# A four-layer GraphSAGE kernel: layer 1's own-feature products made early, one comparison for both one-hot sides, normalisation on VectorE

## The chip, the cores and the metric

The kernel runs on one core of one Trainium2 chip. The metric is device time in microseconds. Four compute engines work side by side, each through its own queue in order: TensorE (PE in the rows; PEld is its weight load), VectorE (DVE), ScalarE (ACT) and GpSimd (POOL). SyncE (SP) issues most of the DMAs. Engines wait for one another through semaphores only.

## The reference, cut to what matters

`x` is 3125 nodes by 256 features in fp32, with 50000 edges (`src`, `dst`), sorted by `dst`.

```python
def _sage_conv(x, src, dst, Wl, Wr, b):
    agg = jax.ops.segment_sum(x[src], dst, num_segments=n)
    deg = jax.ops.segment_sum(jnp.ones_like(dst, dtype=x.dtype), dst, num_segments=n)
    mean = agg / jnp.maximum(deg, 1.0)[:, None]
    return mean @ Wl + x @ Wr + b
h = jnp.maximum(_layernorm(x, axis=-1), 0.0)
h = relu(_sage_conv(h, ..., Wl1, Wr1, b1))      # 256 -> 256
h = relu(_sage_conv(h, ..., Wl2, Wr2, b2))      # 256 -> 128
h = relu(_sage_conv(h, ..., Wl3, Wr3, b3))      # 128 -> 256
return x + _sage_conv(h, ..., Wl4, Wr4, b4)     # 256 -> 256
```

## The kernel before, in words

The nodes lie in 25 tiles of 128; four tiles are a chunk of 512 (six full ones, and a last chunk with 53 nodes, "the tail"). The kernel works through the chunks as seven *places* `q` = 0 to 6, in the order `ORDER` = 5, 6, 4, 3, 2, 1, 0; place 1 is the tail. For each layer and place, TensorE sums the sources: 25 tiles of features `H` (fp16, in two parts, high and low) times a matrix `counts[source, target]` of edge counts, into two banks `agg_ps`, one for each half of the features (L2099, 98 matmuls of 512 columns in a full place).

**Making counts.** `counts` is built while layer 1 runs. Targets are taken in windows; a *step* is up to 128 edges of a window. For each step VectorE compares a row of numbers with the edges' sources (the one-hot `hot_src`, 128 wide) and with a key of target and source tile (`hot_key`, 100 wide for a narrow window, 200 for a wide one): two instructions at L1350 for a group of 4 steps (3 of wide windows). There is room for three groups (`GROUPS`). TensorE multiplies the two (L1928) into one of two window banks, and ScalarE copies each finished window pair into `counts` (L1674). The counts of the chunk of place `q + 1`, or a share of those of the last chunk, are made in place `q`. `script(q)` writes each place's order out for all three engines: a "sum" of one source tile for the first half of the features, a "half" for the second, and the steps spread between them over slots; a layer-1 product ("lin") counts as two slots in which steps may stand.

**Layer 1's linear part.** VectorE scales the sums by the inverse degree into `aggT` (L1444, `scale_agg`). The product of place `q - 1` is made in place `q` (`lin_part`, L1993): for each half `h` of the output two products of `W14[:, 0]` with `aggT` and two of `W14[:, 1]` with `selfT`, all in fp32 and 512 columns wide, in one accumulation in `lin_ps`; a product of 512 fp32 columns shows as two records. `selfT` is the chunk's own features, transposed, which SyncE loads from `hT_d[0]`. ScalarE then applies bias and relu from `lin_ps` (L1715), TensorE makes the narrow product for layer 2 (L2042), and ScalarE and VectorE split that in two parts of fp16.

**Own features.** The seven chunks of x are normalised first. VectorE (chunks in the first four of the order) or ScalarE (the others) makes the moments; ScalarE the root; VectorE `rstd` and `shift` (`h0_shift`); ScalarE one activation per tile, relu(x * rstd + shift) in fp32 in place (`h0_relu`, L1639, 25 tiles), and the high part in fp16 (`h0_high_part`, L1646); VectorE the low part (L1121). TensorE transposes the fp32 features through `ident32` (`h0_turn`, L1891), ScalarE copies them over the chunk's own x in SBUF (`h0_copy`, L1654), and SyncE stores them to `hT_d[0]`. In place 0 the chunks of places 0, 1 and 2 are turned, at tiles 14, 16 and 18; in place 1 the other four. `squares` (L1905), `turn_rows` (L1859) and the rank sums (L1830) also stand in place 0; they prepare bounds of layers 2 to 4 and the late step tables.

**A place's start.** Place `q` begins with the degrees: 100 small matmuls in places 0 and 2 (`add_degrees`, L2121), differences of step keys from place 3 on (`sum_cuts`, L2137). Its first "sum" writes the bank that `scale_agg` of place `q - 1` must have read.

## Time and profile before

| what | value |
|---|---|
| median of 3 runs | 684.47 us (682.58 to 685.35) |
| profiled execution, its own time | 683.4 us |
| its span | 681.6 us |
| mean granted TensorE clock | 0.985 of full speed |
| TensorE busy | 634.0 us, 93% of the span |
| VectorE, ScalarE, GpSimd busy | 283.5, 181.8, 39.1 us |
| the chain that ended last | PE 80%, DVE 10%, ACT 5%, issue 2%, DMA 1% |

All durations of rows are from one profiled execution; its time is 1.07 us under the median of the runs. Layer 1 with everything before it ends at about 327 us of the span; layers 2 to 4 fill the rest. In a row of the timeline, the first number is the start and the second the length; "[idle before <- who]" at its end is how long the engine had nothing to do, and who released it. A matmul's recorded length reaches into the next one, so what one costs is read from the spacing of the starts.

### The profile page before, as it was taken

How to read it: one execution, taken by the hardware profiler on the slowest of the kernel's cores; microseconds unless marked ns; L12 is line 12 of the kernel's file. 1: busy time of each engine (PE TensorE's matmuls, PEld its weight loads, DVE VectorE, ACT ScalarE, POOL GpSimd, SP SyncE). 2: the span in 40 equal slices, each digit the busy share in tenths (PEclk: the TensorE clock that was granted, in tenths of full speed). 3: DMA queues.
4: the chain of work that ended last, by engine and by line, in shares of the span. 5: the costliest groups of instructions: out<-in, count | busy, mean ns of one | idle time of the engine just before them, and what ended most of it. 6: DMA issues, size and time to landing. Idle time of an engine off the chain costs nothing.

```text
span 681.6 us, 10352 instructions
## 1 busy us (share of the span) xinstructions
PE 634.0 (93%) x4071; PEld 346.4 (51%) x4072; DVE 283.5 (42%) x775; ACT 181.8 (27%) x383; POOL 39.1 (6%) x91
## 2 busy tenths in 40 slices
PE   5558888999999999999999999899999999999998
PEld 4234545664554545554454444344445646546586
DVE  6986577478897978822112112121121110101011
ACT  3886882364642622310111110211220000000000
POOL 7000300000000000000000000000001020110110
PEclk9998997799999999999999999899999999999999
DMA  8300020610210111123234351334351123031130
GB/s 264 85 2 3 23 97 3 192 35 7 65 32 4 63 35 63 32 64 103 97 93 124 79 152 48 88 88 109 92 163 38 40 81 109 0 109 44 64 109 32
DMA packets 58727, 49.93 MB, mean 73 GB/s; under 512 B 31222, under 2 KB 44059, under 8 KB 58680
## 3 DMA queue, kind: packets, MB, share of 16 engines
q1 hardware_dynamic: 58324, 48.67, 25.0%
q8 instruction: 32, 0.52, 0.3%
q0 software_dynamic: 240, 0.37, 0.2%
q10 hardware_dynamic: 116, 0.24, 0.1%
q14 instruction: 15, 0.12, 0.1%
HBM read 27.10 MB, written 16.59 MB: 64 GB/s over the span
## 4 chain that ended last, share of the span: by engine, by line
PE 80%; DVE 10%; ACT 5%; issue 2%; DMA 1%; SPq 0%; DVEq 0%; POOL 0%; ACTq 0%; POOLq 0%
PE agg_ps L2099 30%; PE window_ps L2099 18%; PE lin_ps L1993 7%; PE window_ps L1928 6%; PE lin_ps L2017 5%; DVE early L1350 5%; PE lin_ps L2034 5%; ACT counts L1674 2%; PE window_ps L2075 2%; PE agg_ps L2075 2%; PE lin_ps L2042 1%; PE lin_ps L2121 1%; DVE rdeg L1429 1%; DVE aggT L1444 1%; ACT counts L1639 1%
## 5 line engine op out<-in xcount | busy, mean ns | idle before, releaser
L2099 PE MATMUL agg_ps<-counts,H 128*128 128x512 f16 (+3 forms) x1026 | 237.4, 360 | 0.9 <-DVE aggT L1444 0.8
L1350 DVE TENSOR_TENSOR early<-early 128x512 f16<-128x512 bf16 (+2 forms) x466 | 151.9, 389 | 26.5 <-PE window_ps L1928 25.0
L1928 PEld LDWEIGHTS window_ps<-early 128*128 128x128 f16 x892 | 69.6, 100 | 118.4 <-ACT counts L1674 37.1
L1928 PE MATMUL window_ps<-early 128*128 128x100 f16 (+1 forms) x892 | 101.4, 223 | 27.7 <-ACT counts L1674 13.9
L1674 ACT ACTIVATE counts<-window_ps 128x400 f16<-128x400 f32 x196 | 95.9, 504 | 108.5 <-PE window_ps L1928 104.8
L2099 PEld LDWEIGHTS agg_ps<-counts,H 128*128 128x128 f16 (+1 forms) x1026 | 80.8, 99 | 57.7 <-issue 11.0
L2099 PE MATMUL window_ps<-counts,early 128*128 128x512 f16 (+2 forms) x346 | 77.6, 379 | 0.0
L2099 PE MATMUL window_ps<-counts,H 128*128 128x512 f16 (+2 forms) x291 | 55.3, 347 | 0.0
L2099 PEld LDWEIGHTS window_ps<-counts,early 128*128 128x128 f16 (+1 forms) x346 | 33.7, 98 | 41.5 <-issue 3.2
L1452 DVE SCALAR_TENSOR_TENSOR partsT<-newT,columns,partsT 128x512 f16<-128x512 f32 (+1 forms) x21 | 14.4, 683 | 81.6 <-ACT partsT L1729 81.5
L1444 DVE SCALAR_TENSOR_TENSOR aggT<-agg_ps,columns,rdeg 128x512 f32<-128x512 f32 (+1 forms) x27 | 16.9, 658 | 72.7 <-PE agg_ps L2099 66.6
L2099 PE MATMUL agg_ps<-counts,early 128*128 (+4 forms) x297 | 46.5, 315 | 0.0
L2099 PEld LDWEIGHTS window_ps<-counts,H 128*128 128x128 f16 x291 | 24.9, 97 | 29.2 <-issue 1.5
L1715 ACT ACTIVATE newT<-lin_ps,columns 128x512 f32<-128x512 f32 (+1 forms) x28 | 17.3, 632 | 77.0 <-PE lin_ps L2034 45.4
L1031 POOL TENSOR_TENSOR newH<-newH,plan 128x256 f32<-128x256 f32 (+1 forms) x25 | 17.3, 724 | 353.8 <-DMA newH<-in_x_dram 353.8
L2099 PEld LDWEIGHTS agg_ps<-counts,early 128*128 128x128 f16 (+1 forms) x297 | 22.1, 97 | 24.3 <-issue 1.1
L1444 DVE SCALAR_TENSOR_TENSOR aggT<-window_ps,columns,rdeg 128x512 f32<-128x512 f32 (+1 forms) x13 | 9.0, 711 | 56.7 <-PE window_ps L2099 54.5
L1546 DVE TENSOR_TENSOR newT<-lin_ps,newH 128x512 f32<-128x512 f32 (+1 forms) x11 | 7.3, 667 | 51.5 <-PE lin_ps L2017 51.5
L1993 PE MATMUL lin_ps<-aggT,W 128*128 128x512 f32 (+1 forms) x56 | 27.1, 591 | 0.7 <-DVE aggT L1444 0.7
L1993 PE MATMUL lin_ps<-selfT,W 128*128 128x512 f32 (+1 forms) x56 | 25.5, 561 | 0.0
L1729 ACT ACTIVATE partsT<-newT,columns 128x512 f16<-128x512 f32 (+1 forms) x21 | 13.9, 664 | 33.7 <-DMA early<-partsT 18.4
L1715 ACT ACTIVATE newT<-newT,columns 128x512 f32<-128x512 f32 (+1 forms) x7 | 4.7, 667 | 65.8 <-DVE newT L1560 65.8
(218 smaller groups left out, 490.8 us busy)
## 6 DMA issues: line engine op xcount, KB each, us to landing
selfT<-hT_d SPq DMA_DIRECT2D x18, 512.0 KB, 4.3
hT_d<-newT SPq DMA_DIRECT2D x12, 512.0 KB, 4.6
rdeg<-rdeg_d SPq DMA_DIRECT2D x18, 256.0 KB, 4.3
counts<-in_x_dram SPq DMA_DIRECT2D x6, 512.0 KB, 8.1
hT_d<-counts SPq DMA_DIRECT2D x6, 512.0 KB, 3.9
newH<-in_x_dram SPq DMA_DIRECT2D x6, 512.0 KB
out_dram<-newT SPq DMA_DIRECT2D x5, 512.0 KB
hT_d<-newT SPq DMA_DIRECT2D x6, 256.0 KB, 4.0
```

The costliest lines, as they stand in the source:

```text
L1031: nc.gpsimd.tensor_tensor(x4[0:q, i, :], x4[0:q, i, :], b4rows[0:q, :], ALU.add).then_inc(x4_biased, 1)
L1350: last = v.tensor_tensor(hot[:, group % GROUPS, 0:n * size].rearrange("p (r n d) -> p r n d", r=n, d=2), numbers_to[:, 0:size].rearrange(" ...
L1444: v.scalar_tensor_tensor(out=aggT[:, h, 0:n], in0=(agg_ps, window_ps)[bank][:, h, 0:n], scalar=unscale[:, l - 1:l], in1=rdeg[:, 0:n], op0= ...
L1452: v.scalar_tensor_tensor(out=low, in0=(lin_ps if l == 1 else newT)[:, h, 0:n], scalar=scale[:, l - 1:l], in1=partsT[:, 0, 0:n], op0=ALU.mu ...
L1674: a.activation(counts[:, :, 2 * w * WIN:2 * (w + 1) * WIN].rearrange("p t (a w) -> p a t w", a=2), window_ps[:, FILL_AT[w] % 2, 0:2 * KEYS ...
L1715: a.activation(newT[:, h, 0:n], source, ACT.Relu, bias=bT[:, bias + h:bias + h + 1]).then_inc(relu_done[l], 1)
L1928: m(window_ps[:, at % 2, key0:key0 + keys], hot_src[:, group % GROUPS, r * P:(r + 1) * P], hot_key[:, group % GROUPS, r * keys:(r + 1) * k ...
L1993: last = m(lin_ps[:, h, 0:n], W14[:, i // 2, i % 2, h * P:(h + 1) * P], (aggT, selfT)[i // 2][:, i % 2, 0:n], start=(i == 0), stop=(i == 3))
L2017: last = m(lin_ps[0:rows_, g, i * D:(i + 1) * D], h, w, start=(j == 0), stop=(j == len(ops) - 1))
L2034: last = m(lin_ps[:, h, 0:n], w, r, start=(i == 0), stop=(i == len(ops) - 1))
L2075: last = m((agg_ps, window_ps)[bank][:, h, cols], tile[:, part, h * P:(h + 1) * P], counts[0:rows_, k, c * CH + g * HALF_CH:c * CH + (g + ...
L2099: last = m((agg_ps, window_ps)[bank][:, h, 0:n], tile[:, part, h * P:(h + 1) * P], counts[0:rows_, k, chunk_cols(c, n)], start=first and p ...
```

## The change

1. *Own products early.* `own_products(j)` makes the two-by-two products of `W14[:, 1]` with the own features right after the chunk is turned and copied: turn (tiles 1, 5, 9, 13, 17 of place 0), `h0_copy`, products (tiles 3, 7, 11, 15, 19), `own_copy` back over the chunk in SBUF, store. Places 0 to 4 of the order go in place 0, through `lin_ps`; the last two in place 1, through the window banks and `degree_ps`/`turn_bank`. `hT_d[0]`, and so `selfT`, now hold the mapped features.
2. `lin_part` keeps only the two products per half with `aggT`. VectorE adds the loaded `selfT` (`add_own`, at tile 4), writing `newT`; ScalarE's relu reads `newT`, a tile later than before.
3. *One comparison.* For narrow windows, source and key one-hots are both 128 wide and made by one instruction. From place 2 to place 4 (`SPREAD_FROM` to `SPREAD_TO`) they lie in rows of `counts` that belong to the last chunk, 8 steps in a group; elsewhere 4.
4. `ahead(q + 1)` makes the first two groups of places 3 and 4 before `scale_agg` of the place ahead of them.
5. *Normalisation.* VectorE makes x * rstd + shift per tile as one `tensor_scalar`; the relu is taken in the later readers (high part, low part, copy of the turned features).
6. `squares` and some small work is spread over other tiles; the degrees of place 0 must be read from `lin_ps` before the first turn.

```diff
+    SPREAD = 8
+    SPREAD_FROM = steps_of([w for q in range(-1, 2) for w in FILLS[q]])
+    SPREAD_TO = steps_of([w for q in range(-1, NCH - 2) for w in FILLS[q]])
...
-            if q == 1 and k in FIRST_LIN_K:
-                work += [("lin", 4 * FIRST_LIN_K.index(k) + j) for j in range(4)]
+            if q == 1 and k == FIRST_LIN_K:
+                work += [("lin", j) for j in range(4)]
             if q > 1 and k == LIN_K:
-                work += [("lin", j) for j in range(8)]
+                work += [("lin", j) for j in range(4)]
...
-        H0_TURN_K = (14, 16, 18)
-        SQUARES_K = (9, 10, 11)
+        IN_LIN = 5
+        H0_TURN_K, OWN_K = (1, 5, 9, 13, 17), (3, 7, 11, 15, 19)
+        SQUARES_K = (8, 11, 13)
...
-        H0_LATE_K = (1, 4, 7, 10)
+        H0_LATE_K, OWN_LATE_K = 1, (4, 5)
...
+                for i in range(t):
+                    v.tensor_scalar(x_in[c][:, i, :], x_in[c][:, i, :], rstd[:, c, i:i + 1], shift[:, c, i:i + 1],
+                                    ALU.mult, ALU.add).then_inc(h0_made, 1)
...
+            def ahead(q):
+                at = hots_after(q - 1)
+                for _ in range(GROUPS - 1):
+                    if SPREAD_FROM <= at < min(SPREAD_TO, hots_after(q)):
+                        step(*STEP_PAIR[at])
+                        at += HOTS[GROUP_OF[at]][1]
...
+                if wide < WIN:
+                    pairs = numbers_to[:, 0:P].rearrange("p (n d) -> p n d", d=2)
+                    v.tensor_tensor(
+                        hots_of(group).rearrange("p r a (n d) -> p r a n d", d=2),
+                        pairs.unsqueeze(1).unsqueeze(1).broadcast_to([P, n, 2, P // 2, 2]),
+                        step_both[:, at:at + n, :, :].unsqueeze(3).broadcast_to([P, n, 2, P // 2, 2]),
+                        ALU.is_equal).then_inc(hot_made, 1)
+                    return
...
+            def add_own(q):
+                n, t = size_of(chunk_at(q))
+                dve.wait_ge(self_loaded[1], 16 * (q + 1))
+                if q > 0:
+                    dve.wait_ge(hT_stored[1], 16 * q)
+                    dve.wait_ge(narrow_done, q)
+                for h in range(2):
+                    dve.wait_ge(lin_done[1], 2 * q + h + 1)
+                    v.tensor_tensor(newT[:, h, 0:n], lin_ps[:, h, 0:n], selfT[:, h, 0:n], ALU.add
+                                    ).then_inc(own_added, 1)
...
                     if kind == "summed":
+                        if 1 < q < NCH - 1:
+                            ahead(q + 1)
                         scale_agg(1, q, 0)
...
-            def h0_relu(j, tiles):
-                        a.activation(x_in[c][:, i, :], x_in[c][:, i, :], ACT.Relu, bias=shift[:, c, i:i + 1],
-                                     scale=rstd[:, c, i:i + 1]).then_inc(h0_made, 1)
...
-                    a.activation(x_T[c][:, f, 0:t * P], h0_ps(j)[f][:, 0:t * P], ACT.Copy, scale=1 / H0_SCALE
+                    a.activation(x_T[c][:, f, 0:t * P], h0_ps(j)[f][:, 0:t * P], ACT.Relu, scale=1 / H0_SCALE
                                  ).then_inc(h0T_copied, 1)
+            def own_copy(j):
+                act.wait_ge(own_done, 2 * j + 2)
+                for h in range(2):
+                    a.activation(x_T[c][:, h, 0:n], h0_ps(j)[h][:, 0:n], ACT.Copy).then_inc(own_copied, 1)
...
                 if j > 0:
-                    pe.wait_ge(h0T_copied, 2 * j)
+                    pe.wait_ge(own_copied, 2 * min(j, IN_LIN))
...
+            def own_products(j):
+                pe.wait_ge(h0T_copied, 2 * j + 2)
+                pe.wait_ge(weights_loaded, 16 * NW)
+                for h in range(2):
+                    for k in range(2):
+                        last = m(h0_ps(j)[h][:, 0:n], W14[:, 1, k, h * P:(h + 1) * P], x_T[c][:, k, 0:n],
+                                 start=(k == 0), stop=(k == 1))
+                    last.then_inc(own_done, 1)
...
                 if j == 0:
                     pe.wait_ge(agg_scaled[1], 2 * (q + 1))
-                    pe.wait_ge(self_loaded[1], 16 * (q + 1))
-                h, i = j // 4, j % 4
-                last = m(lin_ps[:, h, 0:n], W14[:, i // 2, i % 2, h * P:(h + 1) * P],
-                         (aggT, selfT)[i // 2][:, i % 2, 0:n], start=(i == 0), stop=(i == 3))
+                h, k = j // 2, j % 2
+                last = m(lin_ps[:, h, 0:n], W14[:, 0, k, h * P:(h + 1) * P], aggT[:, k, 0:n], start=(k == 0),
+                         stop=(k == 1))
```

How the instructions move on TensorE at the start of place 0, before (L2121 the degrees, L2099 sums, L1830 rank sums, L1928 steps):

```order
L2121 MATMUL lin_ps<-newH,counts 128x2 x100
L2099 MATMUL agg_ps<-counts,H 128x512 x8
L1830 MATMUL degree_ps<-counts,newH 128x512 x16
L2099 MATMUL agg_ps<-counts,H 128x512 x14
L1928 MATMUL window_ps<-early 128x200 x3
```

and of the changed program (L2201, L2179, L1895 and L2010 are the same lines; L1956 is the turn, L1968 the own products):

```order
L2201 MATMUL lin_ps<-newH,counts 128x2 x100
L2179 MATMUL agg_ps<-counts,H 128x512 x4
L1956 MATMUL lin_ps<-newH,counts 128x128 x8
L2179 MATMUL agg_ps<-counts,H 128x512 x4
L1895 MATMUL degree_ps<-counts,newH 128x512 x16
L2179 MATMUL agg_ps<-counts,H 128x512 x4
L1968 MATMUL lin_ps<-counts,W 128x512 x4
L2179 MATMUL agg_ps<-counts,H 128x512 x8
L1956 MATMUL lin_ps<-newH,counts 128x128 x2
L2179 MATMUL agg_ps<-counts,H 128x512 x2
L2010 MATMUL window_ps<-early 128x200 x3
```

One turn of eight transposes, one of two (the tail) and four products now stand ahead of the first step.

TensorE in place 1, before (L1891 turns, L1993 products of place 0, L2042 the narrow product):

```order
L1891 MATMUL degree_ps<-newH,counts 128x128 x4
L1891 MATMUL turn_ps<-newH,counts 128x128 x4
L2099 MATMUL agg_ps<-counts,H 128x53 x6
L1993 MATMUL lin_ps<-aggT,W 128x512 x2
L1993 MATMUL lin_ps<-selfT,W 128x512 x2
L2099 MATMUL agg_ps<-counts,H 128x53 x6
L1891 MATMUL window_ps<-newH,counts 128x128 x8
```

and changed (L1956 turns, L2073 products with the sums, L1968 own products, L2122 the narrow product):

```order
L1956 MATMUL window_ps<-newH,counts 128x128 x8
L1956 MATMUL degree_ps<-newH,counts 128x128 x4
L1956 MATMUL turn_ps<-newH,counts 128x128 x4
L2179 MATMUL agg_ps<-counts,H 128x53 x6
L2073 MATMUL lin_ps<-aggT,W 128x512 x4
L2179 MATMUL agg_ps<-counts,H 128x53 x6
L1968 MATMUL window_ps<-counts,W 128x512 x4
L2179 MATMUL agg_ps<-counts,H 128x53 x4
L1968 MATMUL degree_ps<-counts,W 128x512 x2
L1968 MATMUL turn_ps<-counts,W 128x512 x2
L2179 MATMUL agg_ps<-counts,H 128x53 x34
L2122 MATMUL lin_ps<-newT,Wl_sb 128x512 x2
```

The two last chunks are turned together, and their eight own products stand between the products of place 0 and the narrow product that waits for its relu.

VectorE in place 3, around the reading of the degrees, before (L1350 the comparisons, L1423 the degrees, L1429 a quarter of their inverses):

```order
L1423 SCALAR_TENSOR_TENSOR rdeg<-degree_ps,rdeg 128x512
L1350 TENSOR_TENSOR early<-early 128x512
L1350 TENSOR_TENSOR early<-early 128x400
L1350 TENSOR_TENSOR early<-early 128x512
L1350 TENSOR_TENSOR early<-early 128x400
L1350 TENSOR_TENSOR early<-early 128x512
L1350 TENSOR_TENSOR early<-early 128x400
L1429 RECIPROCAL rdeg<-rdeg 128x128
```

and changed (L1393 the comparison, L1507 the added own map):

```order
L1393 TENSOR_TENSOR counts<-early 128x8x256 x5
L1507 TENSOR_TENSOR newT<-lin_ps,selfT 128x512 x2
L1473 SCALAR_TENSOR_TENSOR rdeg<-degree_ps,rdeg 128x512
L1393 TENSOR_TENSOR counts<-early 128x8x256
L1479 RECIPROCAL rdeg<-rdeg 128x128
```

Four instructions of 512 and 400 elements have become one of 2048, and two additions stand in VectorE's queue behind the products of the place.

## Rows read from the trace of the kernel before

**Rows 1.** The page, parts 1 and 2: busy times; granted TensorE clock per fortieth

```profile
PE 634.0 (93%) x4071; PEld 346.4 (51%) x4072; DVE 283.5 (42%) x775; ACT 181.8 (27%) x383; POOL 39.1 (6%) x91
...
PEclk9998997799999999999999999899999999999999
```

**Rows 2.** Busy times by stretch: bounds, length, us (instructions) per engine, clock, DMA

```profile
15.00:47.00 32.00, 16.82 (x85) 6.66 (x86) 27.85 (x100) 26.12 (x65) 0.00 (x0) 1.00 0.26 67
47.00:105.00 58.00, 47.75 (x388) 28.00 (x386) 39.92 (x123) 43.82 (x109) 6.19 (x6) 0.97 0.12 37
105.00:126.00 21.00, 19.68 (x182) 13.27 (x183) 12.22 (x40) 6.69 (x14) 0.00 (x0) 0.84 0.25 90
...
168.00:209.00 41.00, 39.83 (x297) 20.66 (x296) 34.39 (x98) 20.09 (x41) 0.52 (x1) 1.00 0.14 41
...
251.00:292.00 41.00, 39.71 (x306) 21.04 (x305) 34.96 (x102) 10.29 (x20) 0.53 (x1) 1.00 0.15 41
292.00:327.00 35.00, 34.10 (x224) 16.81 (x224) 9.17 (x15) 2.06 (x3) 0.53 (x1) 1.00 0.29 87
```

**Rows 3.** Groups by line and shape: busy us, mean ns, idle before and releaser

```profile
L1674 ACT ACTIVATE counts<-window_ps 128x400 f16<-128x400 f32 x196 | 95.9, 504 | 108.5 <-PE window_ps L1928 104.8
L1350 DVE TENSOR_TENSOR early<-early 128x512 f16<-128x512 bf16 x199 | 83.1, 418 | 25.2 <-PE window_ps L1928 24.2
...
L1350 DVE TENSOR_TENSOR early<-early 128x400 f16<-128x400 bf16 x200 | 72.0, 360 | 0.0
...
L1639 ACT ACTIVATE counts<-counts,newH 128x256 f32<-128x256 f32 x25 | 13.5, 599 | 0.6 <-DVE newH L1112 0.6
...
L1546 DVE TENSOR_TENSOR newT<-lin_ps,newH 128x512 f32<-128x512 f32 x10 | 6.9, 692 | 46.8 <-PE lin_ps L2017 46.8
...
L1654 ACT ACTIVATE counts<-lin_ps 128x512 f32<-128x512 f32 x4 | 2.2, 599 | 0.0
```

**Rows 4.** TensorE's timeline, last place of layer 1: start, us, instructions

```profile
329.17 1.88 PE L1993 MATMUL lin_ps<-selfT,W 128*128 128x512 f32 x4
330.89 1.88 PE L1993 MATMUL lin_ps<-aggT,W 128*128 128x512 f32 x4
```

**Rows 5.** TensorE's timeline in place 0: a full place turned, and what follows

```profile
82.15 1.05 PE L1891 MATMUL lin_ps<-newH,counts 128*128 128x128 f32 x8
83.04 0.59 PE L2099 MATMUL agg_ps<-counts,H 128*128 128x512 f16 x2
```

**Rows 6.** Who waited for whom, 47 to 104 us: total, times, longest

```profile
PEld window_ps L1928 <- ACT counts L1674: 12.6, 14, 2.1
...
PE window_ps L1928 <- ACT counts L1674: 7.4, 7, 1.9
```

**Rows 7.** VectorE's timeline, ends of the first stretch and start of place 0

```profile
35.54 1.23 DVE L1121 TENSOR_TENSOR H<-counts,H 128x1024 f16<-128x1024 f32 x1 [1.53 <-ACT H L1646]
...
46.55 4.29 DVE L1132 TENSOR_SCALAR counts<-counts 98x512 f16<-98x512 f16 x16
50.76 0.15 DVE L1477 TENSOR_SCALAR newH<-lin_ps 128x4 f32<-128x4 f32 x1
```

**Rows 8.** One microsecond of place 0: busy times and granted clock

```profile
64.00:65.00 1.00, 1.00 (x6) 0.44 (x5) 1.00 (x11) 0.81 (x2) 0.00 (x0) 0.50 0.00 0
```

**Rows 9.** TensorE's timeline, place 1: products at half clock

```profile
108.89 3.28 PE L1993 MATMUL lin_ps<-aggT,W 128*128 128x512 f32 x4
112.01 1.88 PE L1993 MATMUL lin_ps<-selfT,W 128*128 128x512 f32 x4
```

**Rows 10.** TensorE's timeline where place 3 begins

```profile
167.67 0.59 PE L2099 MATMUL agg_ps<-counts,H 128*128 128x512 f16 x2
168.94 0.29 PE L1928 MATMUL window_ps<-early 128*128 128x100 f16 x3 [0.68 <-DVE early L1350]
```

**Rows 11.** Line 1350 alone, by stretch: VectorE's busy us and instructions

```profile
168.00:209.00 41.00, 28.46 (x88) 1.00 0.14 41
```

**Rows 12.** VectorE's timeline in place 1: one fp32 tensor and a constant

```profile
107.14 0.29 DVE L1293 TENSOR_SCALAR counts<-counts 128x256 f32<-128x256 f32 x1
```

186 lines of the change are left out of this document (111 added, 75 removed).

## The prediction

> **What bounds the kernel now.** I read the page first: TensorE is busy 634.0 of 681.6 us [rows 1], and its clock is full nearly everywhere. So a gain must come from TensorE work that goes, or from work that moves into its 47 idle us. The table by stretch [rows 2] shows where these lie. The first stretch (15 to 47 us) has TensorE half idle, with VectorE busy 27.85 and ScalarE 26.12 of 32 us: these two bound it, hand in hand. Place 0 (47 to 105) has TensorE busy 47.75 of 58, place 1 19.68 of 21. Places 3 and 5 have it busy 39.83 and 39.71 of 41, place 6 34.10 of 35: here TensorE is the bound. VectorE comes next in places 3 and 5 (34.39 and 34.96 of 41); in place 6 it does little. The waits of place 0 [rows 6] say who holds TensorE there: ScalarE's window copies, 7.4 us in 7 pieces. Last I read the timeline at a place's start [rows 10]: the first step waits 0.68 us for VectorE's one-hots, which were not begun before the sums were scaled.
>
> **What the change does to TensorE's sum of work: nothing.** Four of eight fp32 products per place leave `lin_part` and four own products come in. A group of four records, two products, starts 1.72 us before the next [rows 4], so one product is 0.86 and four are 3.44 us. The tail's four short ones move too, from place 2 to place 0, and cancel. So the question is only how much of 6 x 3.44 = 20.6 us finds idle time.
>
> **First stretch: +0.5 us.** Nine tiles are normalised by VectorE instead of ScalarE. No row shows this instruction. The nearest is one fp32 tile of 256 with a constant, 0.29 us [rows 12]; the other end is the activation it replaces, 0.599 [rows 3]. I take 0.29, the same tile on the same engine: nine cost VectorE 2.6 us, and ScalarE is relieved of nine activations. VectorE's wait of 1.53 us for ScalarE's high part [rows 7] then goes, because that chain loses four activations; 2.6 - 1.5 = 1.1, of which I let other waits hide half. Bounds: -1.5 (the activations were the path) to +3.9 (nine at 0.599 less the 1.5).
>
> **Place 0: +10.6 us.** Added on TensorE: own products of four full chunks, 4 x 3.44 = 13.8, and two more turns of full chunks (five instead of three; one is 0.89 [rows 5]), 1.8; together 15.6. Ahead of the first step two new waits stand in TensorE's queue. The first turn waits for the degrees to be read from `lin_ps`. VectorE reads them at 50.76, behind the 16 comparisons of 4.29 us [rows 7], and now four normalisations (1.2) stand ahead of those: I take 0.9 us, since the sums of tile 0 cover the rest. Everything of TensorE's place is queued behind it. The first products wait for `h0_copy(0)`, 2 x 0.6 [rows 3], which stands behind ScalarE's copy of the ranks: 0.8 after the four sums between. So 1.7 us of new waits. Against that stands the old idle: 58 - 47.75 = 10.2 [rows 2], of which 1.9 (the branch over heavy windows at the end) stays, so 8.3. ScalarE gets lighter by 16 activations of 0.54 to 0.6 (9) and heavier by own copies (3.5 pairs, 4) and two more copy pairs (2): it falls from 43.82 to about 41 us over a longer place. The later windows are thus stored in time more often. I let 3.3 of the 8.3 us stay, for the new handshakes turn, copy, product, copy, each some 4 to 5 us of TensorE time apart. The half-clock stretch after the longest gap [rows 8] I take as gone, since products now fill that gap: -1.7. Sum 15.6 + 1.7 + 3.3 - 8.3 - 1.7 = +10.6. Bounds: nothing hidden and the waits on top, 15.6 + 1.7 + 3.3 = 20.6; all idle filled and no waits, 15.6 - 8.3 - 1.7 = 5.6.
>
> The rows show that half clock (0.50, that is 1.2 GHz, against 2.4) at 64 us, a little after the engine had stood still, and it was back soon after dense work [rows 8]. The Trainium skill (TensorE: Matmul & The Clock Gate, "Part 1: The HAM clock gate") says that the throttled clock is the default and activity releases it; by that rule denser place 0 and 1 would run at full clock, and the sum would be better by up to the 1.4 us of the group in [rows 9]; by the row alone place 1 stays as it is.
>
> **Place 1: +2.0 us.** `lin_part` loses 3.44, two own product groups add 6.88, two turns fewer give back 1.8: +1.7. The relu of place 0 moves behind both own copies in ScalarE's queue, and the narrow product waits for it: +0.9. TensorE no longer waits for ScalarE between four single turns: -0.6 (not in the rows, an estimate from the 0.6 of one copy). The half clock stays: four records took 3.12 us there instead of 1.72 [rows 9], after the idle at place 0's end. Bounds 0 to +5.
>
> **Places 2 to 6 and the start of layer 2: -17.2 us.** Products of places 2 to 6 are full ones, halved where TensorE is the bound: five times 3.44 (made in places 3 to 6 and behind place 6). Added behind them is VectorE's `add_own`, an fp32 sum from PSUM like L1546's 0.69 [rows 3], so 1.4 us, then relu and narrow product. In places 3 to 6 some six tiles of sums stand between the products and the narrow one and cover it; at layer 2's start 1.5 us do, and about 0.1 shows. DVE's queue holds steps behind the addition, but up to 24 steps are made ahead, twice as many as before. Cost taken: 0.
>
> **One comparison: VectorE stays under TensorE.** 44 pairs in place 3 took 28.46 us [rows 11], 0.647 a pair. From the two shapes [rows 3], 0.418 - 0.360 us for 112 elements, 0.52 ns each; a pair's 912 elements are 0.474, leaving 0.086 an instruction. One of 2048 is then 1.15 us, 22 of them 25.3: 3.1 less. With 1.4 for the addition VectorE has 34.4 - 3.1 + 1.4 = 32.7 us of work, and TensorE 41 - 3.4 = 37.6. In place 5 groups hold 4 steps: 1024 elements, 0.62, 47 times saves only 1.3, and 35.0 stand against 37.6, with the wait for the last sums besides: I charge 1.0 there. The Trainium skill (VectorE: DVE Perf Modes, "Side-by-side: where the cycles go for N=2048 bf16") gives each instruction a fixed part of some 150 cycles; by it 66 fewer instructions would save some 10 us of VectorE in each of these places. The spacing of the rows shows 0.086 us, so the trace does not bear that out for instructions that follow one another; TensorE's time would not change by either.
>
> `ahead` takes away the 0.68 us of [rows 10] at the starts of places 3 and 4: -1.4. Place 2 has no such help, and its first one-hots are 0.4 us later: +0.4.
>
> **Sum.** 0.5 + 10.6 + 2.0 - 17.2 + 1.0 - 1.4 + 0.4 = -4.1 us. The profiled execution took 683.4, giving 679.3; the median of the runs is 1.07 above it, so 680.4 us.
>
> **Rivals.**
> *Place 0 swallows it all.* ScalarE's relief matters more than I think, all of the old idle is filled, and place 5 is not held: 5.0 less for place 0 and 1.0 for place 5, -10.1, 674.4 us. For it: 8.3 us of idle are there, nearly all of it behind ScalarE [rows 6]. Against: TensorE waits for ScalarE in order, and the copies of own products add new such points.
> *The handshakes serialise (the other side).* Each own product group waits for `h0_copy`, and that stands in ScalarE's queue behind window copies, moments and high parts. If each of the six full groups waits 1.6 us beyond my sum, two window copies and one of the turned ones (2 x 0.504 + 0.6 [rows 3]), this costs 9.6: +5.5, 690 us. The place is TensorE's queue at tiles 7 to 19 of place 0 and 4 and 5 of place 1; it decides from 1.2 us per group on, where 7.5 us cancel the gain and take half a per cent. For it: ScalarE is busy 43.82 of 58 us in place 0. Against: two tiles of sums and steps lie between turn and product.
> *The places become VectorE's.* The halved products don't shorten places 2 to 5 in full, because VectorE is in order and now also waits for the products: a loss of 1.5 in each of four places, +1.9 in all, 686.4, no change. For it: 34.96 of 41 us busy [rows 2].
> *The merged comparison does not keep its rate.* At half of it, 1.04 ns an element, 22 instructions are 48.8 us and the place some 56: four such places cost about 70 us, 750. Against: the innermost pairs are as before.
>
> **Chances.** My forecast 0.40; place 0 swallows it 0.25; handshakes 0.16; VectorE's places 0.16; the comparison 0.03. A measurement of this kernel tells about 0.5%, 3.4 us, from no change; so faster means under 681.1. Of my forecast's own range, 677 to 684, six tenths lie there: 0.24, with 0.25 of the first rival and a little of the third, 0.51. Same: 0.16 of mine and 0.14 of the third, 0.30. Slower: 0.16 + 0.03, 0.19. The range reaches from below the first rival to the handshakes: 672 to 690.
>
> **What would show it.** In the profile after: place 0 10 us longer and TensorE's idle there under 6 us; waits of L1968 for ScalarE's copies small (a sum over 8 us speaks for the handshakes); places 3 and 4 at 37 to 38 us; the 2048-element comparison at 1.2 us; VectorE's normalisation near 0.3 us; no gap at the first step of places 3 and 4; place 6 and the start of layer 2 shorter by 3.4 each; layers 2 to 4 unchanged. It is wrong if place 0 grows by over 16 us or by under 6, or if places 3 to 5 do not shorten by 3 us.

## The result and the profile after

The changed kernel takes 687.91 us (median of 6 runs, 687.37 to 689.92), the kernel before 684.03 (6 runs): a ratio of 1.0067, 95% interval 1.0053 to 1.0081. The whole interval lies above 1, so the change makes the kernel slower. The forecast was 680.4 us and faster. The range, 672 to 690, holds the measured time. The profiled execution took 687.79 us, its span is 686.0. The experiments below were run in four batches; the median of the kernel before, 22 to 30 runs in each batch, stayed at 683.7 to 683.9 us, so medians of different batches can be compared.

The page of the changed kernel, parts 1 and 2, where [rows 1] stood:

```profile
PE 635.7 (93%) x4071; PEld 348.0 (51%) x4072; DVE 292.3 (43%) x547; ACT 176.4 (26%) x372; POOL 40.8 (6%) x91
...
PEclk9999999989999999999999999899999999999999
```

TensorE does the same work in as many matmuls. VectorE is busy 8.8 us longer with 228 instructions fewer. So the 4.4 us of span must have come through place, order or clock, and the table by stretch says where. First the kernel before, cut at the starts of places 0 to 2 (their first degree matmuls) and then at the scalings that end places 2 to 6 and the first of layer 2 (columns as in [rows 2]):

```profile
46.67:104.95 58.28, 48.03 (x394) 28.27 (x395) 40.25 (x124) 44.09 (x109) 6.19 (x6) 0.97 0.12 37
104.95:125.89 20.94, 19.62 (x178) 13.21 (x179) 12.11 (x40) 6.69 (x14) 0.00 (x0) 0.84 0.24 88
125.86:166.77 40.91, 40.15 (x403) 24.66 (x403) 30.34 (x95) 19.87 (x42) 0.00 (x0) 0.92 0.21 53
166.77:208.02 41.25, 40.01 (x297) 20.67 (x296) 34.64 (x97) 20.09 (x41) 0.52 (x1) 1.00 0.14 41
208.02:250.11 42.09, 40.02 (x295) 20.87 (x294) 34.85 (x97) 18.98 (x38) 0.52 (x1) 1.00 0.13 40
250.11:291.67 41.56, 40.37 (x312) 21.39 (x311) 35.52 (x103) 10.29 (x20) 0.53 (x1) 1.00 0.15 41
291.67:325.72 34.05, 33.23 (x222) 16.60 (x222) 8.22 (x14) 2.06 (x3) 0.53 (x1) 1.00 0.30 89
325.72:354.36 28.64, 27.92 (x156) 13.24 (x155) 5.04 (x8) 3.51 (x5) 0.00 (x0) 1.00 0.31 94
354.36:681.60 327.24, 320.44 (x1656) 174.07 (x1654) 46.67 (x76) 25.42 (x40) 17.33 (x25) 0.99 0.30 83
```

and the changed kernel at the same events:

```profile
46.77:122.27 75.50, 65.84 (x450) 37.28 (x450) 46.16 (x119) 42.27 (x107) 7.26 (x6) 1.00 0.09 28
122.27:144.23 21.96, 19.97 (x169) 12.47 (x170) 13.41 (x42) 6.75 (x14) 0.00 (x0) 0.92 0.33 123
144.20:184.01 39.81, 38.91 (x395) 23.55 (x395) 30.85 (x33) 19.94 (x42) 0.00 (x0) 0.91 0.14 33
184.01:221.92 37.91, 36.76 (x289) 19.65 (x288) 33.76 (x33) 20.17 (x41) 0.52 (x1) 1.00 0.16 44
221.92:260.07 38.15, 36.72 (x287) 19.48 (x286) 31.09 (x31) 18.88 (x38) 0.53 (x1) 1.00 0.14 44
260.07:300.15 40.08, 37.15 (x304) 19.84 (x303) 35.95 (x57) 10.35 (x20) 0.52 (x1) 1.00 0.16 42
300.15:330.76 30.61, 29.79 (x214) 15.05 (x214) 9.61 (x15) 2.13 (x3) 0.53 (x1) 1.00 0.33 100
330.76:356.10 25.34, 24.71 (x147) 11.61 (x146) 6.42 (x10) 3.57 (x5) 0.00 (x0) 1.00 0.33 106
356.10:686.00 329.90, 321.98 (x1656) 175.10 (x1654) 46.67 (x76) 25.42 (x40) 17.34 (x25) 0.99 0.30 82
```

| stretch | before | after | difference | forecast |
|---|---|---|---|---|
| up to place 0 | 46.67 | 46.77 | +0.1 | +0.5 |
| place 0 | 58.28 | 75.50 | +17.2 | +10.6 |
| place 1 | 20.94 | 21.96 | +1.0 | +2.0 |
| places 2 to 6, start of layer 2 | 228.5 | 211.9 | -16.6 | -17.2 |
| the rest of layers 2 to 4 | 327.24 | 329.90 | +2.7 | 0 |

Two rows miss by much: place 0 by 6.6 us, and by 2.7 us a stage that the change does not touch. That stage lasted 327.1 to 330.8 us over the seventeen profiles of this study, kernels with and without own products near both ends, so its 2.7 us are within the scatter of single profiles. So is the 0.1 of the first row: place 0 began at 46.0 to 47.5 us in the fifteen profiles of kernels that have no own products ahead of it. In place 0 the reader is to compare two columns. TensorE's busy time grew by 17.8 us, 48.03 to 65.84. Its idle time, length less busy time, was 10.25 and is 9.66. Next to none of the old idle was filled.

The front of place 0 on TensorE after the change; before, the first step (L1928) stood at 59.96, 13.3 us behind the start of the place:

```profile
50.14 1.89 PE L2179 MATMUL agg_ps<-counts,H 128*128 128x512 f16 x4
52.74 1.97 PE L1956 MATMUL lin_ps<-newH,counts 128*128 128x128 f32 x8 [0.71 <-DVE newH L1541]
54.50 1.91 PE L2179 MATMUL agg_ps<-counts,H 128*128 128x512 f16 x4
56.21 4.79 PE L1895 MATMUL degree_ps<-counts,newH 98*128 98x512 f16 x16
60.83 1.03 PE L2179 MATMUL agg_ps<-counts,H 128*128 128x512 f16 x4
62.75 3.70 PE L1968 MATMUL lin_ps<-counts,W 128*128 128x512 f32 x8 [0.89 <-ACT counts L1713]
```

The first step now comes at 68.66. The turn takes 1.76 us here (52.74 to 54.50) and 0.89 later in the place [rows 5]; the 16 rank sums (L1895) take 4.62 us, where they took 3.52 before. The turn is slow at this spot in every profile that has it there. The rank sums are not slow because of the turn: they took 3.45 to 4.62 us in the six profiles with a turn ahead of them and 3.45 to 4.65 in the eleven without. The own products (eight records, four products) take 3.54 us, since the next sum starts at 66.29: 0.1 more than the four products of [rows 4].

TensorE's waits in place 0 after, which answer to [rows 6]:

```profile
PE window_ps L2010 <- ACT counts L1741: 4.9, 5, 2.4
PE lin_ps L2201 <- issue: 1.6, 1, 1.6
PE lin_ps L1968 <- ACT counts L1713: 1.3, 2, 0.9
PE lin_ps L2201 <- ACT counts L1741: 1.2, 1, 1.2
PE lin_ps L1956 <- DVE newH L1541: 0.7, 1, 0.7
PE lin_ps L1956 <- ACT counts L1722: 0.7, 2, 0.4
PE lin_ps L1968 <- issue: 0.2, 1, 0.2
```

(Its columns are the total, the times and the longest.) Window waits fell from 7.4 us behind ScalarE and 1.0 behind VectorE to 4.9; the new handshakes of turns and products cost 2.9 (1.3 + 0.7 + 0.7, and 0.2 of issue). The two rows of L2201 are the degrees at the start and end of the place; the kernel before has them too, 1.2 and 1.7.

The price of VectorE's new instructions, in the groups by line and shape:

```profile
L1393 DVE TENSOR_TENSOR counts<-early 128x2048 f16<-128x2048 bf16 x65 | 77.5, 1215 | 6.5 <-PE window_ps L2010 6.3
...
L1143 DVE TENSOR_SCALAR counts<-counts,newH 128x256 f32<-128x256 f32 x25 | 8.9, 416 | 0.3
```

The comparison of 2048 elements takes 1.2 us on the mean, and 22 of them in place 3 have 26.3 us for the 25.3 forecast. The normalisation (L1143) is 0.416 on the mean; four of them in a row took 1.38, 0.35 a piece, not 0.29.

### The profile page after: what moved, and what is told of

Read it like the earlier page. It is cut to its first block, busy times and chain, and to the rows that moved or that the text cites. A ratio compares the mean times of both kernels' runs of the same rounds, so it can differ in the third digit from the quotient of the medians.

```text
span 686.0 us, 10095 instructions
## 1 busy us (share of the span) xinstructions
PE 635.7 (93%) x4071; PEld 348.0 (51%) x4072; DVE 292.3 (43%) x547; ACT 176.4 (26%) x372; POOL 40.8 (6%) x91
## 4 chain that ended last, share of the span: by engine, by line
PE 81%; DVE 10%; ACT 5%; issue 2%; POOL 1%; DMA 1%; SPq 0%; DVEq 0%; ACTq 0%; POOLq 0%
PE agg_ps L2179 30%; PE window_ps L2179 19%; PE window_ps L2010 5%; PE lin_ps L2097 5%; PE lin_ps L2114 5%; PE lin_ps L2073 3%; PE lin_ps L1968 2%; ACT counts L1741 2%; DVE early L1400 2%; PE lin_ps L2122 2%; DVE early L1393 2%; PE window_ps L2155 2%; PE agg_ps L2155 2%; PE degree_ps L1895 1%; DMA early<-partsT 1%
## 5 line engine op out<-in xcount | busy, mean ns | idle before, releaser
L2179 PE MATMUL agg_ps<-counts,H 128*128 128x512 f16 (+3 forms) x1026 | 238.8, 359 | 0.9 <-DVE aggT L1494 0.8
L2179 PEld LDWEIGHTS agg_ps<-counts,H 128*128 128x128 f16 (+1 forms) x1026 | 80.2, 99 | 59.8 <-issue 14.1
L1393 DVE TENSOR_TENSOR counts<-early 128x2048 f16<-128x2048 bf16 x66 | 78.4, 1211 | 6.5 <-PE window_ps L2010 6.3
L2179 PE MATMUL window_ps<-counts,early 128*128 128x512 f16 (+2 forms) x346 | 77.6, 379 | 0.0
L2010 PE MATMUL window_ps<-early 128*128 128x100 f16 (+1 forms) x366 | 47.0, 238 | 23.1 <-DVE early L1400 13.0
L2010 PEld LDWEIGHTS window_ps<-counts 128*128 128x128 f16 x526 | 40.3, 99 | 48.7 <-issue 9.8
L2010 PEld LDWEIGHTS window_ps<-early 128*128 128x128 f16 x366 | 28.8, 101 | 60.3 <-ACT counts L1741 25.5
L2010 PE MATMUL window_ps<-counts 128*128 128x100 f16 x526 | 52.6, 211 | 3.1 <-ACT counts L1741 2.0
L2179 PE MATMUL window_ps<-counts,H 128*128 128x512 f16 (+2 forms) x291 | 55.3, 347 | 0.0
L2179 PEld LDWEIGHTS window_ps<-counts,early 128*128 128x128 f16 (+1 forms) x346 | 33.6, 98 | 41.5 <-issue 3.2
L1393 DVE TENSOR_TENSOR early<-early 128x1024 f16<-128x1024 bf16 (+1 forms) x69 | 43.8, 681 | 17.8 <-PE window_ps L2010 17.4
L2179 PE MATMUL agg_ps<-counts,early 128*128 (+4 forms) x297 | 46.5, 315 | 0.0
L2179 PEld LDWEIGHTS window_ps<-counts,H 128*128 128x128 f16 x291 | 24.9, 97 | 29.2 <-issue 1.5
L1787 ACT ACTIVATE newT<-newT,columns 128x512 f32<-128x512 f32 (+1 forms) x21 | 13.4, 663 | 89.9 <-DVE newT L1628 65.8
L2179 PEld LDWEIGHTS agg_ps<-counts,early 128*128 128x128 f16 (+1 forms) x297 | 22.1, 97 | 24.3 <-issue 1.1
L2073 PE MATMUL lin_ps<-aggT,W 128*128 128x512 f32 (+1 forms) x56 | 25.1, 564 | 0.6 <-DVE aggT L1494 0.6
```

What stands on the lines that cost most here:

```text
L1393: v.tensor_tensor(hots_of(group).rearrange("p r a (n d) -> p r a n d", d=2), pairs.unsqueeze(1).unsqueeze(1).broadcast_to([P, n, 2, P // 2 ...
L2010: m(window_ps[:, at % 2, key0:key0 + keys], one_src, one_key, start=(j == 0), stop=(j == STEPS[w] - 1)).then_inc(hot_used, 1)
L2073: last = m(lin_ps[:, h, 0:n], W14[:, 0, k, h * P:(h + 1) * P], aggT[:, k, 0:n], start=(k == 0), stop=(k == 1))
L2179: last = m((agg_ps, window_ps)[bank][:, h, 0:n], tile[:, part, h * P:(h + 1) * P], counts[0:rows_, k, chunk_cols(c, n)], start=first and p ...
```

## The experiments

Each ran beside the kernel before. "Place 0" below is the profiled execution's, from one profile each. Two kernels with the TensorE order of the kernel before showed 61.2 us there at a mean clock of 0.94 instead of 58.28 at 0.97, so single profiles of place 0 are sure to some 3 us only; the medians decide.

**e1, part 1 undone.** `lin_part` with eight products again, turns at 14, 16, 18, no `own_products`, `own_copy` and `add_own`; parts 3, 4 and 5 stay.

```diff
-                work += [("lin", j) for j in range(4)]
+                work += [("lin", j) for j in range(8)]
...
-        H0_TURN_K, OWN_K = (1, 5, 9, 13, 17), (3, 7, 11, 15, 19)
+        H0_TURN_K = (14, 16, 18)
...
-                        own_products(OWN_K.index(k))
...
-                        add_own(q - 1)
```

> The changed kernel with its part 1 undone: own products again in lin_part (eight products a place), turns at tiles 14, 16, 18 of place 0, relu from lin_ps; the one comparison, the groups made ahead and the normalisation on VectorE stay. Theory A (place 0 takes the moved TensorE work at its full price, and the other parts are nearly neutral): place 0 is back at 58 to 60 us instead of 75.5, places 3 and 4 end up 0.7 shorter each than in the kernel before, all in all 682 to 684 us, 4 to 6 under the changed kernel. Theory B (the loss is VectorE's: nine normalisations more in the first stretch, four ahead of the degrees, the larger comparisons): place 0 stays at 63 us or more and the whole at 686 to 689. Theory C (the prediction's own sum for the rest: first stretch +0.5, place 5 +1.0, ahead -1.4, place 2 +0.4, front waits none): 684.5.

Measured: 681.25 us (12 runs), ratio to before 0.9967 (0.9946 to 0.9989). Place 0 is 57.07 us:

```profile
47.46:104.53 57.07, 48.26 (x394) 28.50 (x395) 45.56 (x118) 36.77 (x93) 6.39 (x6) 0.97 0.12 37
```

Theory A holds, and its numbers were a little too high: 681.25 for 682 to 684, 57.07 for 58 to 60. Part 1 costs 6.7 us (687.91 - 681.25), more than the whole loss, and the other parts gain 2.6. From scaling to scaling places 3 and 4 took 40.24 and 40.74, 1.0 and 1.3 under the kernel before, place 5 41.34.

**e2, half of each own product left out.** The kernel computes the own map from 128 of the 256 features.

```diff
-                    for k in range(2):
-                        last = m(..., W14[:, 1, k, ...], x_T[c][:, k, 0:n], start=(k == 0), stop=(k == 1))
+                    last = m(..., W14[:, 1, 0, ...], x_T[c][:, 0, 0:n], start=True, stop=True)
```

> The changed kernel with half of each own product left out (the second 128 of the 256 features; two products instead of four per chunk). Everything else, copies and waits too, is as changed. It takes 1.77 us from each of six full chunks: 7.1 in place 0, 3.5 in place 1. Theory A (nothing in place 0 covers the own products): place 0 falls from 75.5 to about 68.4, place 1 by 3 to 3.5, the whole by 10 to 677.5. Rival (the products stand in idle time that comes back when they go): place 0 falls by less than 4, the whole to 681 or more.

Measured: 677.16 us, 10.75 under the changed kernel for 10.6 of work taken out. This median of 6 runs is sure to some 2 us only (ratio to before 0.9916, 0.9884 to 0.9948). The profile is sharper: place 0 is 68.11 us, 7.4 shorter for 7.1 taken out, and TensorE's idle time in it is 9.76 us, where it was 9.66. Theory A: this work had no cover that can be seen. The waits show why. TensorE's timeline of the changed kernel, two of the rows that begin with a wait:

```profile
62.75 3.70 PE L1968 MATMUL lin_ps<-counts,W 128*128 128x512 f32 x8 [0.89 <-ACT counts L1713]
...
94.35 0.22 PE L2010 MATMUL window_ps<-early 128*128 128x100 f16 x1 [2.35 <-ACT counts L1741]
```

and of e2:

```profile
62.49 1.98 PE L1967 MATMUL lin_ps<-counts,W 128*128 128x512 f32 x4 [0.89 <-ACT counts L1713]
...
90.22 0.22 PE L2009 MATMUL window_ps<-early 128*128 128x100 f16 x1 [2.36 <-ACT counts L1741]
```

The waits are the same to a hundredth of a microsecond, and so are those of 0.89, 0.35, 0.33, 0.37, 0.44 and 0.61 us between and behind them. One is not: 0.72 us for a window copy at 114.37 became 0.46, and 0.41 for VectorE came ahead of it. If TensorE's work had been filling time in which ScalarE was behind, less of it would have made the waits longer by some 7 us. All but one of them don't depend on how much TensorE does. My reading: what it waits for begins only after an instruction of its own.

**e3, the first turns later**, the first one behind the rank sums; ScalarE's copies follow.

```diff
-        H0_TURN_K, OWN_K = (1, 5, 9, 13, 17), (3, 7, 11, 15, 19)
+        H0_TURN_K, OWN_K = (3, 6, 9, 13, 17), (5, 8, 11, 15, 19)
```

> The changed kernel with the first two turns and own products later: turn of place 0's chunk at tile 3 (behind the rank sums) instead of 1, its products at 5 instead of 3, the tail's at 6 and 8 instead of 5 and 7. Theory A (the front loses by a wait of 0.7 us and by half speed that lasts longer: the turn took 1.76 instead of 0.89, the 16 rank sums 4.6 instead of 3.4): eight sums and 16 rank sums run as in the kernel before, first step at 65.5 to 66 us instead of 68.66, the whole 2.5 to 3 us faster, 685. Rival (the front's length is the work that stands in it, and ScalarE's burst behind the rank sums only moves): within 0.7 us of the changed kernel, 687.5.

Measured: 687.09 us, ratio to before 1.0050 (1.0031 to 1.0070). TensorE's timeline at the front of place 0:

```profile
50.15 3.59 PE L2179 MATMUL agg_ps<-counts,H 128*128 128x512 f16 x8
...
58.79 1.04 PE L1956 MATMUL lin_ps<-newH,counts 128*128 128x128 f32 x8
...
65.25 0.42 PE L2010 MATMUL window_ps<-early 128*128 128x200 f16 x3
```

The turn is back at 0.87 us, both waits are gone and the first step stands at 65.25, 3.4 earlier. The rank sums still took 4.39 us, where theory A had them as before, at 3.5. But the place ends only 0.6 earlier (74.92 us): behind the front TensorE waits 6.2 us for window copies instead of 4.9, and some half clock comes in (mean 0.98). The front was short as theory A has it, but not by the faster rank sums; the gain was given back, and the time is the rival's.

**e4, ScalarE's queue in another order**: `h0_copy(0)`, five moment pieces and a root ahead of `first_rows`, which waits for the ranks.

```diff
-   2: (h0_root(4), first_rows(3, ...), h0_copy(0)),
+   2: (h0_root(4), h0_copy(0), h0_moment(5, 1), h0_moment(5, 2), h0_moment(5, 3),
+       h0_root(5), h0_moment(6, 0), h0_moment(6, 1), first_rows(3, ...)),
```

> The changed kernel with ScalarE's queue in another order in place 0: the copy of the first turned chunk and six moment pieces stand ahead of the rank row, for which ScalarE waited 10.3 us; TensorE's order is as changed. Theory A (TensorE's waits in place 0 are bursts of ScalarE's queue behind that wait): the 0.9 us wait of the first own products goes, the 2.35 us wait near 94 us shrinks, together 1.5 to 3 us faster, 685 to 686.5. Rival (those waits come from windows finishing one after the other and not from the burst): only the 0.9 goes and half of it comes back, 687 to 688.

Measured: 686.76 us, 1.0042 (1.0024 to 1.0059), between the two. The wait of 0.9 went; the one of 2.35 stayed (2.36), against theory A. Place 0 was 72.44 us, 3.1 shorter, but this profile is of the fastest of 12 executions (682.15 us), and 1.65 of the 3.1 are busy time: the half speed at the front ended sooner (rank sums in 3.45 us with the turn where it was). What ScalarE did in the wait of 2.35, in the changed kernel:

```profile
91.49 1.06 ACT L1705 ACTIVATE H<-counts 128x1024 f16<-128x1024 f32 x1
92.44 0.42 ACT L1687 ACTIVATE counts<-counts 128x256 f16<-128x256 f32 x1
...
92.98 0.51 ACT L1689 ACTIVATE counts<-counts 128x256 f16<-128x256 f32 x1
...
93.61 0.30 ACT L1698 ACTIVATE newH<-counts 128x4 f32<-128x4 f32 x1
93.82 0.88 ACT L1741 ACTIVATE counts<-window_ps 128x400 f16<-128x400 f32 x2
```

A high part, a moment piece and a root stand between two window copies at tile 13, and e4 had left them there.

**e15, one piece out of that burst.**

```diff
-   10: lambda: h0_copy(2), 12: ...,
-   13: lambda: (norms(2), h0_high_part(5), h0_moment(6, 3), h0_root(6)),
+   10: lambda: h0_copy(2), 11: lambda: h0_moment(6, 3), 12: ...,
+   13: lambda: (norms(2), h0_root(6), h0_high_part(5)),
```

> The changed kernel with one edit in ScalarE's queue of place 0: a moment piece (1.25 us) from tile 13 to tile 11, and the root ahead of the high part, so that the burst between two window copies is shorter by the piece. Theory A (the wait is the length of the burst): the 2.35 us wait near 94 us becomes 1.1, every other wait keeps its length, place 0 is 1.2 shorter (74.3). Rival (it is only moved to tile 11): place 0 stays at 75.5.

TensorE's timeline of e15:

```profile
93.01 0.22 PE L2010 MATMUL window_ps<-early 128*128 128x100 f16 x1 [1.19 <-ACT counts L1741]
```

Measured: 686.02 us, 1.9 under the changed kernel; place 0 74.10. The 2.35 became 1.19, less by the piece, and each of the other waits kept its length to 0.05 us. So this wait is as long as the burst in ScalarE's queue; for the shorter ones that was not tried one by one.

**e13 and e14, the bursts out of place 0**, with and without own products: moments ahead of the rank row and at tiles 5 and 7 (without own products: all of them around the rank row), `square_weights` on VectorE at tile 4 instead of 6; in e13 the turns as in e3.

```diff
-   4: lambda: (h0_low_part(3), h0_shift(4)), 6: square_weights,
+   4: lambda: (h0_low_part(3), h0_shift(4), square_weights()),
...
-   13: lambda: (norms(2), h0_high_part(5), h0_moment(6, 3), h0_root(6)),
+   13: lambda: (norms(2), h0_high_part(5)),
```

> The changed kernel with the bursts of place 0 spread: all moment pieces but two and a root ahead of the rank row in ScalarE's queue, the last two pieces at tiles 5 and 7, so that at tile 13 only the high part stands between two window copies; VectorE squares the weights at tile 4, while it waits for the ranks; the first turn and its products behind the rank sums. Theory A (TensorE's idle in place 0 is set by the order of the other queues, and is taken away piece by piece): the 2.35 us wait falls to about 0.8, the front as in the run with the later turn, 683 to 685, 3 to 5 under the changed kernel. Rival (waits are shared out anew): 686 to 687.5.

> The changed kernel with its part 1 undone, and the same spreading of ScalarE's moments and of the squared weights. Its place 0 showed waits of 1.42 and 0.36 us behind the squared weights on VectorE, 1.91 behind ScalarE's high part with a moment piece and a root. Theory A: both shrink to under 0.6, 2 to 3 us less than without the moves (680.9): 678 to 679. Part 1 in e13 still costs 4 or more against this run, since its work lies on the path wherever it stands in place 0. Rival (the bursts were what made part 1 expensive): e13 comes within 2 us of this run.

Measured: e13 683.88 us (ratio 1.0002, 0.9983 to 1.0020), e14 677.53 (6 runs, 0.9909, 0.9878 to 0.9941). Both times are theory A's, e14's even a little below its range; the waits shrank less than it says. In e13 the 2.35 became 1.00 and a new one of 1.53 us for a window copy stands at 68.43; in e14 e7's 1.91 became 1.00, its 1.42 is gone, and VectorE is waited for 1.09 us at 84.06. e14's place 0 is 53.48 us long, against 57.07 in e1, and of these 3.6 us only 2.0 are idle time. The other 1.6 are busy time: the mean clock of the place is 1.00 instead of 0.97, so the half clock that e1 has behind its waits is gone. Reordering was worth 4.0 us with the own products and 3.7 without (681.25 - 677.53). Part 1 still costs 6.4 (683.88 - 677.53): not the bursts made it dear. e14 is the fastest kernel of the study that does the whole work, 0.9% under the one before and 1.5% under the changed one.

**e7**, an early form of e14 with three moment pieces and a root moved only.

```diff
-   2: (h0_root(4), first_rows(3, ...)),
+   2: (h0_root(4), h0_moment(5, 1), h0_moment(5, 2), h0_moment(5, 3), h0_root(5), first_rows(3, ...)),
```

> The changed kernel with its part 1 undone, as in the first run of this study (681.25 us), and ScalarE's three moment pieces and a root moved ahead of the rank row for which it waits. Theory A (window waits of place 0 are bursts of ScalarE behind that wait): 1 to 3 us less than that run, 678.5 to 680. Rival (waits there come from the windows' own rhythm): 681 within 0.7.

Measured: 680.88 us (0.9965, 0.9946 to 0.9984), 0.4 from e1: the rival's number. It had left the burst at tile 13 and the squared weights in place, and the waits of 1.91 and 1.42 behind them.

**e5 and e6, own products ahead of place 0**, between the windows of the first stretch, where TensorE was half idle: two places' (e5), three places' (e6).

```diff
+        EARLY = 2
+        EARLY_TURN = {17: 0, 25: 1}
+        EARLY_OWN = {19: (0, 0), 20: (0, 1), 21: (0, 2), 22: (0, 3), 27: (1, 0, 1, 2, 3)}
-        H0_TURN_K, OWN_K = (1, 5, 9, 13, 17), (3, 7, 11, 15, 19)
+        H0_TURN_K, OWN_K = (9, 13, 17), (11, 15, 19)
...
+                    pe.wait_ge(own_copied, 2 * EARLY)
```

The keys are windows, the numbers behind them places and products. Both also have ScalarE's moments ahead of the rank row, as e4 has.

> The changed kernel with the own products of the first two places of the order (one full chunk and the tail) moved ahead of place 0, between the windows of the first stretch, where TensorE stood idle for 15 of 32 us; the full chunk's four products one by one behind four windows. ScalarE's queue in place 0 as in the run with another order, less these copies. Theory A (place 0 has no cover, the first stretch has): place 0 loses a turn of 0.9, products of 3.5, the tail's 1.1, and with them the wait and the half speed of the front (about 2.8), 8 us in all against the changed kernel's, first stretch at most 1 us longer: 679 to 680.5. Rival (the first stretch hangs on VectorE and ScalarE hand in hand, and each burst of TensorE pushes the windows back): the stretch grows by 3 or more, 683 or more.

> As the run with two early places, with the third place's chunk too (turn behind window 26, its four products behind windows 28 to 31). Theory A: another 0.9 + 3.5 = 4.4 us from place 0, first stretch up to 1.5 longer for the last products, since little stands behind them: 675.5 to 677.5. Rival: its products and copies stand where nothing covers them and the degrees wait for the copy: no gain over the run with two, 679 to 682.

Measured: e5 686.09 us (1.0035, 1.0022 to 1.0048), e6 684.94 (1.0020, 1.0000 to 1.0040). Place 0 began at 51.32 and 55.20 us instead of 46.77, and lasted 70.7 and 63.0. Of the 4.8 and 12.5 us by which place 0 was shorter, 4.5 and 8.4 came back in the first stretch. e5 went the rival's way. e6 lies above both expectations, since neither allowed for so long a stretch. New waits stood there too, in e5 1.40 us for the copy of the turned chunk, and turns took 1.54 us. Half clock came on top: in e5 the granted clock was 0.50 from 44 to 59 us, and the mean of place 0 was 0.89 (e6: 0.95) instead of 1.00. What of the miss is order and what is clock was not separated. That TensorE's idle in that stretch is of the same kind as in place 0, a waiting for others that wait for it, fits the runs and is not shown by them alone.

**e8, the addition of the own map cut to 4 of 512 columns from place 2 on.**

```diff
-   v.tensor_tensor(newT[:, h, 0:n], lin_ps[:, h, 0:n], selfT[:, h, 0:n], ALU.add
+   v.tensor_tensor(newT[:, h, 0:4 if q > 1 else n], lin_ps[:, h, 0:4 if q > 1 else n], ...
```

> The changed kernel with the addition of the own map cut to 4 of 512 columns for the places from 2 on: 1.2 us less of VectorE in each of places 3 to 6 and at the start of layer 2. Theory A (place 5 is VectorE's, places 3 and 4 are not): place 5 (40.1 us from scaling to scaling) shortens by 1.0 to 1.3, places 3 and 4 (37.9 and 38.2) by less than 0.4, start of layer 2 by 0.5 or less: 686 to 686.7. Rival (places 3 and 4 hang on VectorE too): each shortens by 1, 684.5.

Measured: 687.31 us. Place 5 took 39.02 us instead of 40.08, places 3 and 4 37.91 and 38.01 instead of 37.91 and 38.15. So place 5 hangs on VectorE, places 3 and 4 do not: theory A. The whole is 0.6 under the changed kernel where 1.2 to 1.9 were expected, which a median of 7 runs doesn't settle. Its place 0, where nothing was changed, was 76.68 us in this profile and 75.50 in the changed kernel's.

**e12, parts 3 and 4 alone**, normalisation on ScalarE.

> The kernel before with parts 3 and 4 alone: the one comparison, groups of 8 from place 2 to place 4, two groups made ahead; normalisation stays on ScalarE. Theory A (the 2.6 us by which the kernel without own products is faster than the one before come from the starts of places 3 and 4 and from fewer waits for comparisons): 681 to 682. Rival (half of it is ScalarE's relief by the normalisation on VectorE, in place 0): 682.5 to 683.5.

Measured: 682.78 us, 0.9987 (0.9970 to 1.0004). From place 3 to place 6 its lengths are e1's within 0.01 us (40.23, 40.74, 41.34, 34.05), so the gain of places 3 and 4 is parts 3 and 4. The whole is the rival's number. The 1.5 us between e12 and e1 would then be part 5's, but the two intervals overlap, and the mean clock of place 0 (0.94 against 0.97) may be all of it: what part 5 is worth was not shown.

**The gap in layer 3.** The 2.7 us of the last row of the table come from one place, the tail of layer 3, on TensorE before and after:

```profile
438.01 0.42 PE L2034 MATMUL lin_ps<-aggT,plan 128*128 128x53 f32 x2 [3.14 <-DVE aggT L1444]
```

```profile
440.93 0.67 PE L2114 MATMUL lin_ps<-aggT,plan 128*128 128x53 f32 x2 [4.66 <-DVE aggT L1494]
```

TensorE waits for VectorE, VectorE for ScalarE's high part, and that for the DMA transposition of the part before, which took 8.89 us before (from 431.40) and 10.41 after (from 432.80). Half clock follows the gap, 3.4 us of it before and 6.8 after. e9, e10 and e11 are e1, the changed kernel and the kernel before with VectorE's scaling of the tail put ahead of the low part that waits for that high part.

```diff
-                    scale_agg(l, q, bank)
+                    if not (l == 3 and q == 1):
+                        scale_agg(l, q, bank)
...
                     for h in range(TURNS[l]):
+                        if l == 3 and q == 0 and h == 1:
+                            scale_agg(3, 1, 1 - bank)
                         low_part(l, q, h)
```

> The changed kernel with its part 1 undone, and in layer 3 the scaling of the tail's sums ahead of the second low part of the first place in VectorE's queue (behind it, it waits for a DMA transposition: TensorE stood still for 3.1 to 4.7 us there and then ran at half clock for 3 to 7 us, in every profile so far). Theory A (TensorE's gap there hangs on that place in VectorE's queue alone): gap gone and with it most of the half clock, 4 to 6 us less than without the swap (681.25): 675.5 to 677.5, and runs that lie closer together. Rival (something behind it waits for the same DMA, so the gap only moves): 680 or more.

> The changed kernel with the same swap in layer 3. Theory A (of the measured loss of 3.9 us, layer 1 and the start of layer 2 account for 1.7, and the rest is this gap, which fell out 1.5 us longer with more half clock): 682 to 684, and 1.2 to 2.4 above the kernel before with the same swap. Rival (the gap is as long in both kernels over many runs; the loss lies elsewhere): the distance to the kernel before with the swap stays at 3.5 or more.

> The kernel before with the same swap in layer 3. Its gap was 3.14 us and the half clock behind it took some 1.6 more. Theory A: 4 to 5 us less than the kernel before, 679 to 680.5. Rival (the gap only moves): 683.5.

Measured: 681.75, 690.54 and 685.12 us (ratios 0.9968, 1.0089, 1.0007). The gap moved to the next instruction that needs the same DMA, TensorE's turn of the tail, and grew: 5.1, 6.4 and 5.0 us. Theory A falls in all three, and with it my reading that 2.7 of the 4.4 us were this gap's accident: with the swap the changed kernel is 5.4 us above the kernel before, not the 1.2 to 2.4 expected (e10's profile has half clock in place 6, worth 1.7 us, see below; it would not close the distance). Over the profiles of this study the first transposition took 8.9 to 9.3 us in five kernels (before, e2, e4, e9, e11) and 10.1 to 10.6 in the other twelve, with and without own products in both kinds. What decides between the two stays open.

## Why the prediction was wrong

**The step that failed** is place 0, forecast +10.6 us and measured +17.2, and it failed in two terms: 2.7 of the 6.6 us are idle time that was not filled, 3.9 are work.

*The idle time.* "I let 3.3 of the 8.3 us stay" treated TensorE's idle of place 0 as room: ScalarE is behind, so more TensorE work lets it catch up. Measured, idle went from 10.25 to 9.66 us, where the sum (less 8.3, plus 3.3 kept, plus 1.7 of new waits) has 7.0. e2 shows that the moved products had no cover, and e15 that the longest wait there is as long as the burst that stands in ScalarE's queue between two window copies. Window waits did fall, by 3.5 us, and 2.9 of handshakes took their place.

*The work.* The sum had 15.6 us less 1.7 of half clock, 13.9; busy time grew by 17.8. The first turn at half speed is 0.9 of the difference. The tail's own products are another 0.9, which the prediction let cancel against place 2 (place 2 is indeed 1.1 shorter). The products' 3.54 instead of 3.44 are 0.4. The slower rank sums are 1.1, but that is luck of these two profiles and not the change: with and without a turn ahead of them they took 3.5 to 4.6 us. That leaves 0.6 unaccounted. The 1.7 of half clock at 64 us did go, as forecast: the clock is 1.00 there. But the prediction looked for half speed only where [rows 8] recorded it; at the front of the place, into which the first turn moved, the spacing of the first eight sums shows it (below).

**Front waits:** 0.9 and 0.8 were forecast, 0.71 and 0.89 measured. The half speed of the turn behind the first was missed.

**First stretch:** +0.1 for +0.5, although an instruction cost 0.35 and not 0.29. The same first stretch was 0.7 us longer in e1's profile, so this agreement says little.

**Place 1:** +1.0 for +2.0. Its mean clock is 0.92 instead of 0.84, where the prediction kept [rows 9]'s half clock.

**Places 2 to 6 and layer 2's start:** -16.6 for -17.2 (with 1.0 and -1.4 and 0.4 in it). Place 6 and the start of layer 2 gave 3.44 and 3.30, place 4 3.94 for 4.1, place 3 3.34 for 4.1. Against e1 the halved products gave places 3 and 4 only 2.3 and 2.6 each. TensorE's busy time fell by 2.8 and 2.9 there, not 3.4, and its idle time grew by 0.5 and 0.3: two waits for window copies of 0.56 and 0.42 stand in place 3, where e1 has one of 0.40 for VectorE. Place 4 has the same two, but e1 has two of 0.42 and 0.50 there as well. Why the busy time fell by less was not looked into.

Place 6 was luck in part. In four of the ten profiles with the own products made early (e3, e10, e13, e15) it lasted 32.30 us instead of 30.61, with the same waits: the clock fell to half behind a long run of matmuls of four columns (L2217), and TensorE had stood still only for the 0.82 us at the place's start that all ten have. Without early own products it was 34.04 or 34.05 us at full clock in all seven. Part 1 gives 3.4 us back there in some executions and 1.7 in others. The same six microseconds of place 6, in the tables by stretch, first in the changed kernel, then in e15:

```profile
312.00:318.00 6.00, 6.00 (x27) 2.83 (x26) 2.73 (x4) 0.00 (x0) 0.00 (x0) 1.00 0.65 222
```

```profile
311.14:317.14 6.00, 6.00 (x23) 2.43 (x22) 2.73 (x4) 0.00 (x0) 0.00 (x0) 0.75 0.67 223
```

Place 5 gave 1.5 for 2.4, VectorE's bound as forecast but larger:

```profile
PE window_ps L2010 <- DVE early L1393: 2.5, 5, 0.9
```

Those are TensorE's waits for VectorE between 260.07 and 300.15; in the same place of e1 they are 0.8 us.

**The comparison and `ahead`:** right. The 42 comparisons of 2048 elements of places 3 and 4 (two more are made ahead, in place 2) took 49.6 us, 1.18 each for 1.15 forecast, and the gaps of [rows 10] are gone there; in e1, without part 1, the two places are 1.0 and 1.3 shorter for 0.7 each.

**The rivals.** "Place 0 swallows it all" is the forecast's error made larger. "The places become VectorE's" came nearest in time (686.4), and that is luck: its mechanism is true of place 5 alone, as e8 shows. "The handshakes serialise" came next (690), and its mechanism is not what happened either: 2.9 us of such waits in place 0, where its sign was a sum over 8. That the range holds the measured time is owed to the handshake rival's number alone. What was missing is the plainest rival: that work added to place 0 costs its full price. On the sum of the prediction, with none of the old idle filled, that is 8.3 - 3.3 = 5.0 us more, 685.4.

**Why moved work costs at all.** By the medians part 1 costs 6.7 us (after against e1) and 6.4 (e13 against e14). By the two profiles of after and e1 it is 18.4 more in place 0 and 0.8 in place 1, and 13.8 less behind (0.9, 2.3, 2.6, 1.3, 3.4 and 3.3 in places 2 to 6 and at the start of layer 2): 5.4. In these two profiles the rows account for it: places 3 to 5 gave back 6.2 of the 10.3 us that left them (+4.1), the handshakes are 2.9, the half speed at the front 2.0; against that stand 2.0 less of window waits (4.9 after, 6.9 in e1) and 1.7 less of half clock. Sum 5.3. Of the front's 2.0 only the turn's 0.9 belongs to part 1. Over the whole span the two profiles are 3.9 us apart and the medians 6.7: e1's profile is of the slowest of its 12 executions, and place 6 is at full clock in both. So the medians give the size of part 1's cost, the profiles its kinds, and how much each kind has of the 6.7 stays open.

## What to carry to other kernels

Idle time of an engine is room only if what it waits for would go on without it. Look at what its releaser did in the gap: where that is a burst between two of the releaser's own duties, begun after the waiter's last instruction, more work for the waiter fills nothing, and the burst is what to move. Leaving half of an added piece of work out and comparing the waits one by one tells the two apart in a single experiment.

## What the runs showed of the hardware that was not expected

*Half speed that the clock column does not show.* Behind the 100 degree matmuls of two columns, eight sums of 512 columns took 3.39 us before, 0.42 a piece, while the granted clock of these microseconds is recorded as 1.00; the sixteen rank sums behind them, up to 56.94, took 0.22 a piece. In e5 the same eight sums, where the clock is recorded as 0.50, took 3.38. TensorE's timeline of the kernel before:

```profile
50.03 3.60 PE L2099 MATMUL agg_ps<-counts,H 128*128 128x512 f16 x8
53.42 3.68 PE L1830 MATMUL degree_ps<-counts,newH 98*128 98x512 f16 x16
```

One microsecond of it in the table by stretch:

```profile
51.00:52.00 1.00, 1.00 (x4) 0.32 (x3) 1.00 (x2) 0.25 (x1) 0.00 (x0) 1.00 0.00 1
```

TensorE's timeline of e5:

```profile
54.83 3.59 PE L2199 MATMUL agg_ps<-counts,H 128*128 128x512 f16 x8
```

The same sums in its table by stretch:

```profile
54.83:58.21 3.38, 3.38 (x9) 1.18 (x9) 3.35 (x12) 3.19 (x12) 0.00 (x0) 0.50 0.17 54
```

In the changed kernel a gap of 0.71 us and a turn stand in this stretch, and rank sums were still slow at 56 us. How long the slow stretch lasts changes from one profile to the next (rank sums in 3.45 to 4.65 us). The Trainium skill (TensorE: Matmul & The Clock Gate, "Part 1: The HAM clock gate") has the engine start throttled and released by activity; the spacing agrees with that, the recorded clock does not, so spacing of like matmuls is the surer reading.

*Half clock without a gap.* The half clock of place 6 in four profiles (above) came while TensorE had been busy for 9 us, behind matmuls of four columns; in six profiles of kernels with the same TensorE order in that place it did not come. What decides it was not found.

*Scatter.* Runs of the kernel before took 678.7 to 686.9 us. The five fastest of 110, up to 679.9, had the highest mean clock, 0.992, and most of the others 0.982 to 0.987; but six with only 0.965 or 0.967 took 683.0 to 685.7, so the mean clock alone does not tell a run's time. Place 0 was 58.3 us in one profile and 61.2 in two others with the same TensorE order (mean clock 0.97 and 0.94). Places 3 and 4 agreed to 0.02 us between profiles of the same TensorE and VectorE order.
